# New instruction order on VectorE, in the head, the last pair and the tail, and first loads issued by ScalarE beside SyncE

## The reference

```python
x = x + attn(layernorm(x))      # 16 heads of 128, rotary on q and k, causal window of 128, then @ wo
x = x + ffn(layernorm(x))       # w1: 256 -> 1024, w2: 1024 -> 256
# attn
q, k, v = h @ wq, h @ wk, h @ wv
q, k = rotary(q), rotary(k)
p = softmax(where(k_pos > q_pos - 128 and k_pos <= q_pos, q @ k.T / sqrt(128), neg))
out = (p @ v) @ wo
# ffn, weights rounded to -1, 0, 1 by a scale: clip(round(w / mean(abs(w))), -1, 1)
y = gelu(h @ w1q.T + b1) @ w2q.T + b2
```

## Time and profile before

| | |
|---|---|
| median of 3 runs | 381.81 us (381.13 to 382.01) |
| the profiled execution | 381.72 us, its span 379.7 us |
| mean granted TensorE clock | 0.973 of full |
| PE busy | 348.8 us (92%) |
| PEld | 322.2 us (85%) |
| DVE | 265.8 us (70%) |
| POOL | 223.9 us (59%) |
| ACT | 207.6 us (55%) |

### The profile page before, as it was taken

One profiled execution on the slowest core, in us unless ns is written; L12 is line 12 of the kernel. 1 busy time (PEld: TensorE's weight loads), 2 busy tenths in 40 slices (PEclk: granted clock), 3 DMA queues, 4 the chain that ended last, 5 costly groups with the idle time before them and its releaser, 6 DMA issues.

```text
span 379.7 us, 6922 instructions
## 1 busy us (share of the span) xinstructions
PE 348.8 (92%) x2410; PEld 322.2 (85%) x2410; DVE 265.8 (70%) x607; ACT 207.6 (55%) x626; POOL 223.9 (59%) x182
## 2 busy tenths in 40 slices
PE   6878889999999999999999999999979986579996
PEld 6767669999889999999999999999869986576986
DVE  5776767667668877888788767766847743649682
ACT  2335665676775556656655665666526651236270
POOL 2318677766566778988899766777645650041200
PEclk9899999999999999999999999999989998869999
DMA  7465555443332433333333333333212310000011
GB/s 218 115 160 146 140 152 154 114 97 85 81 73 72 102 93 85 84 85 83 85 83 85 85 88 90 93 90 87 56 28 58 83 29 0 2 1 0 2 55 55
DMA packets 29025, 31.25 MB, mean 82 GB/s; under 512 B 3392, under 2 KB 20288, under 8 KB 28992
## 3 DMA queue, kind: packets, MB, share of 16 engines
q1 hardware_dynamic: 28992, 30.82, 32.1%
HBM read 12.98 MB, written 1.05 MB: 37 GB/s over the span
## 4 chain that ended last, share of the span: by engine, by line
PE 61%; DVE 14%; ACT 12%; DMA 4%; SPq 3%; issue 2%; POOL 1%; DVEq 0%
PE PR L376 16%; PE OT L451 10%; PE VO L408 10%; PE VO L391 8%; PE SC L426 8%; DMA swapped<-by_sin 3%; PE PT L437 3%; ACT probs L587 2%; DVE gT_lo L755 2%; ACT probs L580 2%; ACT gT_hi L575 2%; PE VO L498 2%; DVE probsT L748 2%; DVE SC L734 1%; DMA v_raw<-in_wv 1%
## 5 line engine op out<-in xcount | busy, mean ns | idle before, releaser
L917 POOL TENSOR_TENSOR gT_lo<-turn,gT_hi 128x512 fp32r<-128x512 f32 x62 | 81.9, 1321 | 54.2 <-ACT gT_hi L575 53.9
L912 POOL TENSOR_TENSOR turn<-turn,swapped 128x512 f32<-128x512 f32 x62 | 80.2, 1293 | 32.4 <-DMA swapped<-by_sin 32.3
L580 ACT ACTIVATE probs<-SC,negmax 128x128 f32<-128x128 f32 x128 | 45.9, 363 | 81.2 <-DVE negmax L737 81.2
L755 DVE TENSOR_TENSOR gT_lo<-OT,gT_hi 128x256 fp32r<-128x256 f32 x64 | 27.2, 425 | 76.8 <-ACT gT_hi L599 76.6
L451 PE MATMUL OT<-probsT,v_sb 128*128 128x128 f32 x480 | 66.7, 282 | 8.0 <-DVE probsT L748 8.0
L451 PEld LDWEIGHTS OT<-probsT,v_sb 128*128 128x128 f32 x480 | 60.6, 196 | 10.9 <-DVE probsT L748 10.8
L376 PE MATMUL PR<-xT_hi,qk_lo 128*128 128x512 f32 x128 | 55.9, 436 | 4.7 <-POOL qk_lo L899 3.2
L587 ACT ACTIVATE probs<-probs,rinv 128x128 f32<-128x128 f32 x128 | 44.5, 395 | 25.0 <-DVE rinv L742 24.9
L376 PE MATMUL PR<-xT_hi,qk_hi 128*128 128x512 f32 x128 | 51.0, 398 | 0.0
L376 PE MATMUL PR<-xT_lo,qk_hi 128*128 128x512 f32 x128 | 50.5, 394 | 0.0
L748 DVE TENSOR_TENSOR probsT<-PT,mask_sb 128x512 f32<-128x512 f32 x64 | 43.6, 681 | 3.5 <-PE PT L437 3.5
(11 more groups left out here) (114 smaller groups left out, 838.7 us busy)
## 6 DMA issues: line engine op xcount, KB each, us to landing
swapped<-by_sin SPq DMA_DIRECT2D x128, 128.0 KB, 2.3
qk_raw<-in_wq SPq DMA_DIRECT2D x16, 128.0 KB, 2.6
qk_raw<-in_wk SPq DMA_DIRECT2D x16, 128.0 KB, 2.8
v_raw<-in_wv SPq DMA_DIRECT2D x8, 256.0 KB, 3.0
o_raw<-in_wo SPq DMA_DIRECT2D x8, 256.0 KB, 2.9
xres<-in_x SPq DMA_DIRECT2D x4, 256.0 KB, 3.4
w_raw<-in_w1t SPq DMA_DIRECT2D x4, 256.0 KB, 3.2
w_raw<-in_w2t SPq DMA_DIRECT2D x4, 256.0 KB, 3.0
```

What stands on the lines that cost most here:

```text
L580: nc.scalar.activation(probs[n % 2][:, i], SC[n % 2][:, i * 256 + P:(i + 1) * 256], ACT.Exp, bias=negmax[:, n % 2, i:i + 1], accum_out=row ...
L755: tt(oT_lo(head)[:, ts], OT[:, 0:256], oT_hi(head)[:, ts].bitcast(F32), ALU.subtract).then_inc(otlo_done, 1)
L912: tt(turn[m % 4][:], turn[m % 4][:], swapped[m % 2][:], ALU.add).then_inc(rot_done, 1)
L917: tt(rot_lo(head, c % 2)[:, half_of(c)], turn[m % 4][:], rot_hi(head, c % 2)[:, half_of(c)].bitcast(F32), ALU.subtract).then_inc(rotlo_don ...
```

## The change

Loads: ScalarE issues identity, head 0's weights, the values' weights and head 1's weights; SyncE the four pairs of x tiles, then sine and cosine of each half, now with a semaphore for each table. In the head, values 0 and 1 are projected ahead of the second half's transposes; GpSimd's `qklo(0)` waits for the first four normalised tiles and `qklo(1)` stands behind `rotate(2)`. In the loop `ot_lo(n-2)` stands behind `merge(n)` and `mask_pt(n-1)`; the thresholds are made at the end of step 20; head 15's weights are split one step earlier. In the last pair the order of output projections is 24, 25, 28 and 29, 26, 27, then 30 and 31 among the ffn1 products; `add_out` stands ahead of `inverse_sum` there; `transpose_x(1, 0)` and two ffn1 products stand ahead of the last transposes of probabilities. The arithmetic is the same.

```diff
         def fills(n):
 
             if n >= LP:
-                return ((("v", 4 * PAIRS - 3),), (("v", 4 * PAIRS - 2),), (("v", 4 * PAIRS - 1),),
-                        (("o", 4 * PAIRS - 8),), (("o", 4 * PAIRS - 7), ("o", 4 * PAIRS - 6)),
-                        (("o", 4 * PAIRS - 5), ("o", 4 * PAIRS - 4)), (("o", 4 * PAIRS - 3),), ())[n - LP]
+                e = 4 * PAIRS
+                return ((("v", e - 3),), (("v", e - 2),), (("v", e - 1),), (("o", e - 8),), (("o", e - 7),),
+                        (("o", e - 4), ("o", e - 3)), (("o", e - 6),), (("o", e - 5),))[n - LP]
+            if n < 2:
+                return (("v", n + 2),)
...
-                return (("v", 4 * p + s + 1),)
+                return (("v", 4 * p + s + 1),) if p > 0 else ()
...
 # SyncE
             for i in range(2):
                 sp.dma_start(xres[:, 2 * i:2 * i + 2], xv[:, 2 * i:2 * i + 2]).then_inc(x_in[i], 16)
-            load_head(0)
-            sp.dma_start(ident_sb[:], ident).then_inc(ident_in, 16)
...
-            load_tables(0)
-            load_v(0)
-            load_head(1)
-            load_tables(1)
+            load_table(0, sin_sb)
+            load_table(0, cos_sb)
+            load_table(1, sin_sb)
+            load_table(1, cos_sb)
             swap(0)
-            swap(1)
...
+            swap(1)
             swap(2)
...
 # TensorE
             project(0, 0)
             project(1)
+            project_v(0)
+            project_v(1)
             transpose_x(0, 1)
-            project_v(0)
             project(2, KD)
...
                 fill(n)
+                if n == STEPS - 1:
+                    transpose_x(1, 0)
                 if n > 0:
                     weigh_v(n - 1)
-            project_out(4 * PAIRS - 2)
-            transpose_probs(STEPS - 1)
-            transpose_x(1, 0)
-            weigh_v(STEPS - 1)
             ffn1(0)
             ffn1(1)
+            transpose_probs(STEPS - 1)
+            ffn1(2)
+            weigh_v(STEPS - 1)
+            ffn1(3)
+            project_out(4 * PAIRS - 2)
+            ffn1(4)
             project_out(4 * PAIRS - 1)
-            for k in range(2, NF):
+            for k in range(5, NF):
                 ffn1(k)
...
 # ScalarE
+            act.dma_start(ident_sb[:], ident).then_inc(ident_in, 16)
+            load_head(0)
             nc.scalar.preload_act_table(ACT.Exp)
+            act.dma_start(v_raw[:], wv.rearrange("(k p) n -> p k n", p=P)[:, :, 0:2 * HD]).then_inc(v_in, 16)
+            load_head(1)
             qkhi(0)
+            xt_hi(0, 0)
             vhi(0)
-            xt_hi(0, 0)
+            copy_v(0)
+            xt_hi(0, 1)
+            copy_v(1)
+            rothi(0)
             qkhi(1)
-            xt_hi(0, 1)
-            copy_v(0)
-            rothi(0)
...
                 exps(n)
+                if n == STEPS - 1:
+                    xt_hi(1, 0)
+                    ot_hi(n - 1)
+                    nc.scalar.preload_act_table(ACT.Gelu)
...
-                if s == 5 and p < PAIRS - 1:
+                if s == (4 if p == PAIRS - 2 else 5) and p < PAIRS - 1:
                     qkhi(2 * p + 3)
...
-                if s == 3 and p == PAIRS - 1:
+                if s == 2 and p == PAIRS - 1:
                     ohi(p)
...
             for k in range(2 * NF):
                 gelu(k)
+                if k == 1:
+                    ot_hi(STEPS - 1)
...
 # VectorE, head
             normalise(0, 0)
-            for t in range(4, NT):
-                tile_stats(0, t)
+            tile_stats(0, 4)
+            tile_stats(0, 5)
+            xt_lo(0, 0)
+            tile_stats(0, 6)
+            tile_stats(0, 7)
             moments(0, 1)
-            xt_lo(0, 0)
+            dve.wait_ge(sin_in[0], 32)
+            times_sin(0)
+            dve.wait_ge(cos_in[0], 16)
+            times_cos(0)
             normalise(0, 1)
...
 # VectorE, loop
             for n in range(STEPS):
-                if n >= 2:
-                    ot_lo(n - 2)
-                merge(n)
-                if n == STEPS - 1:
+                if n == STEPS - 2:
                     add_out(4 * PAIRS - 3)
                     tile_stats(1, 2)
                     tile_stats(1, 3)
-                    moments(1, 0)
+                if n == STEPS - 1:
+                    ot_lo(n - 2)
+                    normalise(1, 0)
+                merge(n)
                 if n > 0:
                     mask_pt(n - 1)
                 if n == MEANS_AT:
-                    thresholds()
+                    mean_sums()
+                if 1 < n < STEPS - 1:
+                    ot_lo(n - 2)
+                if n == STEPS - 2:
+                    moments(1, 0)
                 if n + 4 < CHUNKS:
                     times_sin(n + 4)
+                if n >= LP + 4:
+                    for kind, w in fills(n - 1):
+                        if kind == "o" and w != 4 * PAIRS - 3 and w != 4 * PAIRS - 4:
+                            add_out(w)
                 inverse_sum(n)
...
-                if n == STEPS - 2:
+                if n == STEPS - 3:
+                    add_out(4 * PAIRS - 4)
                     tile_stats(1, 0)
                     tile_stats(1, 1)
+                if n == MEANS_AT:
+                    thresholds()
...
 # GpSimd
             rsqrt(0, 0)
+            pool.wait_ge(xn_ready, 4)
             qklo(0)
             rsqrt(0, 1)
             vlo(0)
-            qklo(1)
             pool.wait_ge(rot_done, 2)
             rotate(2)
+            qklo(1)
             pool.wait_ge(rotlo_done, 2)
...
-                if s == 6 and p < PAIRS - 1:
+                if s == (5 if p == PAIRS - 2 else 6) and p < PAIRS - 1:
                     qklo(2 * p + 3)
...
-                if s == 4 and p == PAIRS - 1:
+                if s == 3 and p == PAIRS - 1:
                     olo(p)
```

More of the change, by code:

```diff
@@ L118, in preln_block_kernel @@
         x_in = [sem(f"x_in{i}") for i in range(4)]
-        tab_in = [sem(f"tab_in{i}") for i in range(2)]
+        sin_in = [sem(f"sin_in{i}") for i in range(2)]
+        cos_in = [sem(f"cos_in{i}") for i in range(2)]
         mask_in = sem("mask_in")
@@ L650, in _ @@
                     abs_sums(n - 10)
-            ot_hi(STEPS - 2)
-            nc.scalar.preload_act_table(ACT.Gelu)
-            xt_hi(1, 0)
-            ot_hi(STEPS - 1)
             act.wait_ge(bias_in, 32)
@@ L852, in _ @@
                     ternary(i)
-            normalise(1, 0)
+            xt_lo(1, 0)
+            add_out(4 * PAIRS - 5)
             ot_lo(STEPS - 2)
             mask_pt(STEPS - 1)
-            xt_lo(1, 0)
+            ghi(0)
+            glo(0)
+            ot_lo(STEPS - 1)
+            glo(1)
             add_out(4 * PAIRS - 2)
@@ L859, in _ @@
             tile_stats(1, 5)
-            ot_lo(STEPS - 1)
-            ghi(0)
-            glo(0)
+            ghi(2)
+            glo(2)
             add_out(4 * PAIRS - 1)
@@ L866, in _ @@
             moments(1, 1)
-            glo(1)
-            ghi(2)
-            glo(2)
+            glo(3)
+            ghi(4)
+            glo(4)
             normalise(1, 1)
-            glo(3)
-            for k in range(4, NF, 2):
-                ghi(k)
-                glo(k)
-                glo(k + 1)
+            glo(5)
+            ghi(6)
+            glo(6)
+            glo(7)
             xt_lo(1, 1)
```

41 lines of the change are left out of this document (24 added, 17 removed).

## The result

The changed kernel takes **361.56 us** (median of 4 runs, 360.81 to 362.33); the kernel before, on the same chip, 381.91 us (381.13 to 382.15). The ratio is 0.9471, with a 95% interval of 0.9444 to 0.9497. The forecast was 361.9. The profiled execution took 362.33, its span is 360.3, so 2.0 us lie around it as before.

A forecast was written before the change was run, and what follows sets the result against it. TensorE was taken as the bound, so only places where it stands or runs slow were priced: 1.1 - 2.3 - 5.0 - 13.7 = -19.9 from 381.81 gives 361.9 us, range 358.0 to 368.0.

The forecast's parts named there:

- head, scores(7): Start to step 7: a new wait for head 1's split and half clock make scores(7) 1.1 us later, at 56.7.
- steps 7 to 53: Loop: merge and mask no longer queue behind ot_lo, removing the 2.3 us excess of steps 14 to 20.
- step 54: Late loop: head 15's weights split one step earlier, so the step falls from 9.60 to 4.55, gaining 5.0 us.
- last pair: From 305.81 to the end of ffn2(0): 36.9 us instead of 50.56, a gain of 13.7.
- the x tiles as before: Head: x tiles arrive as before, sharing with identity and head 0 costing 0.2 us; transposes end near 8.6.
- 3.85 per step: Steps 2 to 6, without filling: the time per step used to carry scores(2) at 37.4 to scores(7) at 56.7.
- the walk through VectorE's queue: Last pair: idle times estimated at 0.3 to 0.7 us per VectorE instruction, summing to 6.3 us.
- A: Head: the wait is there but the clock stays up; 2.2 us less, 359.7. Chance 0.10.
- B: Last pair: idles of 1.3 and 0.7 before ffn1(0) drop the clock, two slow stretches; 365.3. Chance 0.20.
- C: Last pair: the Gelu table load stalls ScalarE a second 1.28 us ahead of scale_probs(63); 363.2. Chance 0.12.
- D: Last pair: waits only move, one near 2.5 us with half clock, halving the gain; 369. Chance 0.08.
- E: Every full step: weighing waits for ot_lo behind mask, 0.42 us in some 50 steps; slower, 385. Chance 0.04.

The follow-up runs named there:

- e9_loads_sp: The changed kernel with all first loads issued by SyncE again, in the order of the kernel before: 360.51 us, ratio 0.9476.
- after_again: The changed kernel itself, unedited, run once more on a second chip beside the kernel before: 362.05 us, ratio 0.951.
- e2_warm_wait: The changed kernel with 14 unused keep-warm products filling TensorE's wait ahead of project(4) in step 0: 359.25 us, ratio 0.9436.
- e5_otlo_first: The changed kernel with ot_lo(n-2) ahead of merge(n) again in steps 2 to 55: 365.70 us, ratio 0.9608.
- e4_before_split54: The kernel before with only head 15's cast and split moved one step earlier: 375.22 us, ratio 0.9848.
- e12_before_fills: The kernel before with only the new order of output projections in the last pair, add_out places following it: 376.00 us, ratio 0.9879.

## Why the prediction was right

The forecast of 361.9 lies 0.3 above the median. The terms, with the profiled executions (381.72 and 362.33):

| term | forecast | measured | |
|---|---|---|---|
| head, scores(7) | +1.1 | +2.1 | 57.74 for 56.7 |
| steps 7 to 53 | -2.3 | -2.4 | 215.45 for 217.84; steps 14 to 20 alone -2.0 |
| step 54 | -5.0 | -5.0 | 4.63 for 9.60 |
| last pair | -13.7 | -13.7 | 36.83 for 50.56 |
| behind it | 0 | -0.4 | |
| sum | -19.9 | -19.4 | |

**Head: right in kind, short by 1.0, and closer than its steps deserved.** The step "the x tiles as before" with 0.2 us for sharing failed: statistics began 0.4 to 1.1 us later than the 3.59 of before, and the loads' share of the whole is 1.5 us by `e9_loads_sp`. The rule of the Trainium skill that the prediction set beside its row (DMA: Bandwidth & Descriptors, section "Issuing engines are not separate DMA queues") would have had 0.9 there and was nearer. Projection 0 still began at 11.55 for a forecast 11.3, because seven keep-warm products took 1.73 us and not the 2.67 of the earlier trace rows: a second error, of 0.9, with the other sign. That row was no fixed price: it ran in part at half clock (0.63 from 9.87 to 12.50), and `after_again` has 2.82 for the same products, with projection 0 at 12.40. It matters little, since where they are short TensorE waits 0.99 for v_lo behind them, and in `after_again`, where they are long, that wait is absent. "Scores(0) near 23.2" was 24.30; that is where the late x tiles show. The wait was forecast at 4.0 and measured 3.71, rotate(2) at 25.4 to 26.7 and measured 26.43. The half clock was charged 2.0 and cost 2.5 by this trace and 2.4 by `e2_warm_wait`, but 1.5 by `after_again` (4.46 for 2.92); the 4.3 us at half speed behind the charge's upper end stand in no row that the prediction names. What the prediction did not give a term of its own is ot_lo's new place in steps 2 to 6, 1.0 to 1.9 by `e5_otlo_first`; it was inside the 3.85 per step, which measured 3.81 here and 4.00 in `after_again`.

**Loop: right in mechanism, nearly so in place.** The whole 2.3 was looked for in steps 14 to 20; 2.0 came there and 0.4 in step 21. `e5_otlo_first` puts ot_lo alone at 2.9, more than the change gained there. `e4_before_split54` gives the 5.0 of step 54 as 5.0 by its trace, against this one execution of before.

**Last pair: right in the sum, by two errors.** The idle times came to 4.1 instead of 6.3: most waits were a little shorter than the walk through VectorE's queue said (filling 29: 0.97 for 1.2; ffn1(0): 0.38 for 0.7; ffn2: 0.46 for 1.0) and weighing 62 had 0.38 for 1.3. The work came to 32.8 instead of 30.6: a piece behind a wait is dearer than the chain's price of the same piece without one. The chain has 1.13 to 1.14 for weighing there against 0.89, 1.66 for filling 29 against 1.44, 2.17 for the first two ffn1 against 1.86. These make 1.3 of the 2.2 (three weighings, one filling, the ffn1 pair); where the rest lies was not taken apart. So 2.2 too little work and 2.2 too much waiting met, by luck. The account of before was short of two things as well: it names 1.42, 2.50 and 2.50 of waiting and one fall of the clock, where the trace has a fourth wait of 3.23 and half clock behind the third and fourth too. The term did not suffer, since it was formed from the window's whole 50.56.

**The rivals.** A (clock stays up) did not happen, the window's 0.67 rules it out. B (half clock in the last pair) did not: clock 1.00, the waits of 0.38 before weighing 62 and 0.38 before ffn1(0) were much shorter than the 1.3 and 0.7 it stood on. C (the table load blocks longer) is refuted by the start of scale_probs at 320.85; the 1380 ns of drain that the Trainium skill gives (ScalarE: Activation LUTs, section "What ACT_TABLE_LOAD costs") is not seen here. D: no wait of the last pair is over 1.13. E: weighing does now wait for ot_lo, 2.8 us in seven places, none over 0.5, in steps 2 to 6, which have no filling, and in 60 and 62, which have no projection; in a full step projection and filling cover it, as forecast.

One caution stands beside the agreement. The 13.7 were formed against one execution whose last pair ran at a clock of 0.86. The same stretch at 0.96 in `e4_before_split54` is 3.9 shorter, so against such an execution the term would be 10, and step 54's 5.0 would be 3.4 against that of `e12_before_fills`. Of the 19.4, the clock's share is 5.9 in the last pair and 1.8 in step 54 (9.60 - 3.16 - 4.63), less 2.5 in step 0: 5.2. In the runs of this study the kernel before lies between 378.5 and 384.9 us, with mean clocks of 0.982 and 0.964 at these ends; the changed one lies between 360.8 and 362.3. Not settled is which part of the 4.7 us of idle time left by `e12_before_fills` each further move earns (normalising ahead of merge, the order of ffn1, output projections 30 and 31); only add_out was taken apart, at 0.3.

## What to carry to other kernels

An in-order queue charges a short job with the longest wait in front of it: before moving an instruction, read what its new neighbour waits for. A wait of TensorE of the length seen here, 2.5 to 3.7 us, often costs twice, once as itself and again as half clock, and since the second part comes and goes, one profile's half clock is no fixed price: look at more than one execution before you put it into a sum. And when a second engine issues loads "for free", look at the first instruction that needs data: its bytes may now share the way with others, whatever is saved in issuing.
